# Opening loads issued step by step, ones multiplied on TensorE before the first features, and the last graph's softmax in thirds

## The chip, the cores and the metric

One core of one Trainium2 chip runs the whole program. The metric is the device time of one execution in microseconds (us). Engines are named as in the profile: PE (TensorE matmul) and PEld (its weight loads), DVE (VectorE), ACT (ScalarE), POOL (GpSimd), and SP (SyncE), which here issues every transfer.

## The reference

64 graphs of 128 nodes with 384 features go through four layers, each of the form x = x + layer(relu(layernorm(x))). Layers 0 and 2 are masked self-attention with 6 heads. Layers 1 and 3 are graph attention with 12 heads and a gate:

```python
h = einsum('bnd,ade->bane', feat, W); th = tanh(h)
attn = th @ w_src + swap(th @ w_dst)              # 12 heads, 128x128 each
attn = where(attn >= 0, attn, 0.2 * attn)
attn = softmax(where(adj, attn, -999.0))
out = elu(einsum('banm,bame->bane', attn, h) + b)
gate = sigmoid(feat @ H_w.T + H_b)
out = gate * out + (1 - gate) * feat
```

## The kernel before

A pair of layers (attention, then graph attention) is applied to one graph at a time. There are 2 pairs and 64 graphs, so 128 graph passes (`ALL = 128`), and they are software-pipelined: every engine's program is an unrolled loop over steps k from -7 to 132 (`run_steps`, L221), and in step k each engine does one stage each for graphs k+7 down to k-5. Every engine runs strictly in the order in which its program is written; between engines there are semaphores that count graphs. `r.has(g)` asks whether graph g exists, so the first steps and the last ones hold only some of the stages.

The stages that matter here, with the engine and the line:
- Statistics of the input of graph k+7 on DVE (L617 and L619); inverse deviation of graph k+5 on POOL (`layernorm`, L369); normalised features `hM` of graph k+4 on POOL (L411); their transpose on PE for graph k+5 of the step before (`features`, L721 to L724, called at L836); the high part `hT_hi` on ACT (L549) and the low part `hT_lo` on DVE (L655). DVE's order in step k puts the statistics of graph k+7 ahead of `hT_lo` of graph k+4.
- Queries and keys on PE for two graphs at once (`queries_keys`, L735, called at L771, L797 and L800; nine matmuls each). The first ones, in step -3, wait at L769 for `hT_lo` of graphs 0 and 1.
- Graph-attention scores of graph k-3: PE writes them into PSUM banks 5, 6 and 7, one bank for four heads (L812 to L815). ACT applies the leaky slope to all three banks in one instruction (L525), DVE writes the no-edge score (L636) and takes the maxima of the 12 heads (L640), ACT takes 12 exponentials, four per wait (`graph_exps`, L503, called at L555, L561 and L563), PE transposes them by fours (L787, L792, L805), ACT copies them (L520, L522, L534), and PE multiplies with the features (L862).
- The product goes through a 32x32 transpose on DVE (L652, `gcT`), four transfers to DRAM and one back (`context_back`, L269 to L279), and is then normalised on DVE (L625, two steps later than the scores' step). In step k DVE does: L625 for graph k-5, the reciprocal L632 for graph k-4, L636 and L640 for graph k-3, L652 for graph k-4. In step 130 that is: L625 of graph 125, L632 of 126, mask and maxima of 127, and L652 of 126. In step 131: L625 of 126, L632 of 127, L652 of 127.

Weights come as 14 pieces (`PIECES`, L145) of 192 or 288 KB through 8 staging slots. ACT rounds a piece to its high part (L584) and DVE subtracts to the low part (L692), in the steps of `SPLIT_STEPS` (L153). Pieces 8 to 13 reuse slots, so SP waits before each for the split of the piece eight before it (L250).

SP's opening order is written out at L281 to L302: features of graph 0, the identity, graph 1, pieces 0 to 5, bias columns, the first adjacency half, graph 2, pieces 6 and 7, graph 3, vectors of pair 0 (768 KB), head bias, one 576 KB matrix of pair 0 (`wf_stage[0]`), pieces 8 to 13, features of graphs 4 to 7, the second adjacency half, the matrix and the vectors of pair 1. Only then comes `straight(k)` for k from -2 on (L304, L352). `straight(-2)` waits for the copy of graph 0's features (`xb`, L343) and loads graph 8, `straight(-1)` the same for graphs 1 and 9; `straight(0)` and `straight(1)` send the head bias to DRAM and back. `xb` of graph 0 is POOL's (L406), in its step -1, behind the output bias of pair 0 (L481). PE reads the matrices of pair 0 and of pair 1 in its setup of step -2 and step 1 (L867 to L874).

PE's program starts with a wait for the identity (L710). The memsets of `ones` (a 128x128 tile, bf16) and others are POOL's first instructions (L360 to L367).

Of the kernel before, what the change touches and what calls it, by code (L numbers as in the profile page):

```python
# [32 lines left out]
NEG = -9000000000000000.0  # L33
NO_EDGE = -999.0
SLOPE = 0.2
# [6 lines left out]
HALF_SLOTS = SLOTS // 2  # L42
# [13 lines left out]
def graph_stack(nc, x, adj, w_qk, w_vf, w_hg, b_cols, vecs, h_b, ident, sel_src, sel_dst, out):  # L56
    B = x.shape[0]
    ALL = PAIRS * B

    with ExitStack() as ctx:  # L60
# [3 lines left out]
        def sem(name):  # L64
# [12 lines left out]
        vec = sb("vec", [128, PAIRS, 4, D])  # L77
# [72 lines left out]
                  ("gate", 2, D, COLS), ("gate", 2, D + COLS, COLS),  # L150
                  ("h", 2, 0, COLS), ("h", 2, COLS, COLS)]
        READY = {name: n + 1 for n, (name, _, _, _) in enumerate(PIECES)}
        SPLIT_STEPS = {-4: range(0, 3), -3: range(3, 6), -2: range(6, 8), -1: range(8, 11), 0: range(11, 14)}  # L153

        def whole(name):
# [9 lines left out]
        def bank(i):  # L165
            return psum[:, i, :]

        def banks(i, k):
            return psum[:, i:i + k, :]

        def chunks(ap):
# [9 lines left out]
            "cT_hi", "cT_lo", "o_ps", "x1",  # L181
            "g_stats", "g_mv", "g_var", "g_rstd", "g_shift", "g_h", "g_hT", "g_hi", "g_lo", "g_h_ps", "g_gate_ps",
            "g_th", "g_gate", "g_sigmoid", "g_haug", "g_prod", "g_sd", "g_sd_hi", "g_rest1", "g_sd_mid", "g_rest2", "g_sd3",
            "gc_out", "gc_back", "g_sdT_ps", "g_sdT", "g_sdR", "z_ps", "z_leaky", "z_masked", "z_max", "z_exp0", "z_exp1", "z_exp2",
            "gpt_ps0", "gpt_ps1", "gpt_ps2", "gpt0", "gpt1", "gpt2",
            "gc_ps", "gc", "pv_ps", "pv_rden", "pv_norm", "y_min", "y_exp", "ey_f", "xf", "elu_f", "mixed", "x2")}

# [44 lines left out]
        def _(sp):  # L232
# [3 lines left out]
            def load_x(src, g, slot):  # L236
                sp.dma_start(xin[:, slot:slot + 1, :], src[g:g + 1, :, :].rearrange("b p n -> p b n")).then_inc(x_in[slot], 16)

            def load_adj(g, half):
                sp.dma_start(adj8[:, half * HALF_SLOTS:(half + 1) * HALF_SLOTS, :],  # L240
                             adj[g:g + HALF_SLOTS, :, :].rearrange("b p n -> p b n")).then_inc(adj_in[half], 16)

            def load_piece(m):

                name, region, at, n = PIECES[m % len(PIECES)]
                if m >= len(PIECES) + 4:
                    j = m - len(PIECES) - 4
# [45 lines left out]
            sp.dma_start(vec[:, 0, :, :], vecs[0].partition_broadcast(128)).then_inc(s["vec_in0"], 16)  # L293
            sp.dma_start(hb_row[:], h_b.rearrange("k (a e) -> (k a) e", e=GD)).then_inc(s["hb_in"], 16)
            sp.dma_start(wf_stage[0], w_vf[0][:, D:2 * D].rearrange("(c p) n -> p c n", p=128)).then_inc(s["wf_in0"], 16)
            for m in range(8, len(PIECES)):
                load_piece(m)
            for i in range(4, SLOTS):
                load_x(x, i, i)
            load_adj(HALF_SLOTS, 1)  # L300
            sp.dma_start(wf_stage[1], w_vf[1][:, D:2 * D].rearrange("(c p) n -> p c n", p=128)).then_inc(s["wf_in1"], 16)
            sp.dma_start(vec[:, 1, :, :], vecs[1].partition_broadcast(128)).then_inc(s["vec_in1"], 16)  # L302

            def straight(k):  # L304

                if k == 0:
                    sp.wait_ge(s["hb_step"], 5)
                    sp.dma_start(hb_parts.rearrange("p (a e) -> a p e", e=GD), hb_part[:]).then_inc(s["hb_out"], 16)
                if k == 1:
                    sp.wait_ge(s["hb_out"], 16)  # L310
                    sp.dma_start(hb3[ROWS:ROWS + PARTS, :, :].rearrange("p k n -> p (k n)"), hb_parts).then_inc(s["hb_back"], 16)
                j, odd = divmod(k - AHEAD_STEP, SPREAD)
                if odd == 0 and 0 <= j < len(PIECES):
                    load_piece(len(PIECES) + j)
                if odd == 0 and 3 <= j < len(PIECES) + 3:
                    keep_piece(j - 3)
                for p in range(2):
                    if k == B - 3 + p + -1:
                        for i in [0, 2, 1]:
                            sp.wait_ge(s[f"qk_ps{i}"], B - 1 + p)  # L320
                            load_next(f"c{p}{i}")
                g = k - 4
                if 0 <= g < ALL:
                    context_back(g)
                if k == B - 2:
                    sp.wait_ge(s["m_v"], B)
                    load_next("V")
                g = k + 3
                if g % HALF_SLOTS == 0 and g >= SLOTS and g < ALL:
                    sp.wait_ge(s["masks"], g - HALF_SLOTS)  # L330
                    load_adj(g % B, g // HALF_SLOTS % 2)
                if k == B - 1:
                    sp.wait_ge(s["o_ps"], B)
                    load_next("O")
                g = k - 5
                if 0 <= g < ALL:
                    sp.wait_ge(s["x2"], g + 1)
                    slot = g % SLOTS
# [12 lines left out]

            for k in range(-2, ALL + 5):  # L352
                straight(k)
            for i in range(SLOTS):
                sp.wait_ge(stored[i], 16 * (ALL // SLOTS + 1))
# [137 lines left out]
        def _(act):  # L493
# [23 lines left out]
            def step(r, k):  # L517
# [4 lines left out]
                    act.activation(PTG[:, 1, :], bank(2), ACT.Copy).then_inc(s["gpt1"], 1)  # L522
                if r.has(k - 3):
                    act.wait_ge(s["z_ps"], r.done(k - 3))
                    act.activation(LG[:].rearrange("p (e n) -> p e n", e=3), banks(5, 3), ACT.Prelu, alpha=SLOPE).then_inc(s["z_leaky"], 1)  # L525
                if r.has(k + 2):
                    act.wait_ge(s["qk_ps1"], r.done(k + 2))
                    queries_keys(r, k, 1, bank(1)).then_inc(s["qk1"], 1)
# [22 lines left out]
                    act.wait_ge(s["g_hT"], r.done(k - 1))  # L551
                    act.activation(gT_hi[:], chunks(bank(0)), ACT.Copy).then_inc(s["g_hi"], 1)
                if r.has(k - 3):
                    act.wait_ge(s["z_max"], r.done(k - 3))
                    graph_exps(range(0, 4)).then_inc(s["z_exp0"], 1)  # L555
                if r.has(k):
                    act.wait_ge(s["c_ps"], r.done(k))
                    act.activation(cT_hi[:], chunks(bank(2)), ACT.Copy).then_inc(s["cT_hi"], 1)  # L558
                if r.has(k - 3):
                    act.wait_ge(s["z_max"], r.done(k - 3))  # L560
                    graph_exps(range(4, 8)).then_inc(s["z_exp1"], 1)  # L561
                    act.wait_ge(s["z_max"], r.done(k - 3))
                    graph_exps(range(8, 12)).then_inc(s["z_exp2"], 1)  # L563
                if r.has(k + 1):
                    act.wait_ge(s["m_v"], r.done(k + 1))
# [28 lines left out]
        def _(dve):  # L594
# [4 lines left out]
            def step(r, k):  # L599
# [31 lines left out]
                    wait_latest(dve, r, ("pv_norm", k - 6))  # L631
                    dve.reciprocal(rdenG[:, (k - 4) % 2, :], den[:]).then_inc(s["pv_rden"], 1)  # L632
                if r.has(k - 3):
                    dve.wait_ge(s["z_leaky"], r.done(k - 3))
                    dve.wait_ge(s["masks"], r.done(k - 3))
                    dve.copy_predicated(LG_heads, no_edge[:, (k - 3) % 2, :].unsqueeze(1).broadcast_to([128, GH, N]),  # L636
                                        no_edge_score[:].unsqueeze(2).broadcast_to([128, GH, N])).then_inc(s["z_masked"], 1)
                    dve.wait_ge(s["z_masked"], r.done(k - 3))
                    dve.wait_ge(s["z_masked"], r.done(k - 3))
                    dve.tensor_reduce(neg_max[:, 1, :], LG_heads, AX.X, ALU.max, negate=True).then_inc(s["z_max"], 1)  # L640
                if r.has(k + 1):
                    dve.wait_ge(s["s_ps"], r.done(k + 1))
                    dve.wait_ge(s["bias_mask"], r.done(k + 1))
# [65 lines left out]
        def _(pe):  # L709
# [154 lines left out]
                    last.then_inc(s["gc_ps"], 1)  # L864

            def setup(k):
                for pair, at in ((0, -2), (1, 0)):  # L867
                    if k == at:

                        pe.wait_ge(s[f"wf_in{pair}"], 16)  # L870
                        pe.wait_ge(s["bv_cols"], pair + 1)
                        for c in range(KC):
                            last = pe.matmul(bank(3)[:, 0:D], bv_cols[pair][:, c, :], wf_stage[pair][:, c, :], start=(c == 0), stop=(c == KC - 1))
                        last.then_inc(s["out_bias_ps"], 1)  # L874
                if k == 1:
                    pe.wait_ge(s["hb_back"], 16)
                    pe.nop(nofuse=True)
                if k == 2:
                    pe.wait_ge(s["setup_dve"], 2)
                    pe.nop(nofuse=True)  # L880

            run_steps(step, setup)


# [35 lines left out]
```

## Time and profile before

| what | value |
|---|---|
| median of 3 runs | 2048.41 us (2048.01 to 2048.42) |
| the profiled execution's own time | 2048.47 us |
| its span (first to last instruction of the trace) | 2046.4 us |
| busy share of the span | PE 97%, PEld 90%, DVE 89%, ACT 95%, POOL 80% |
| chain that ended last | ACT 49%, DVE 37%, PE 5% |

The span is shorter than the time by 2.07 us, which is what lies around the first and the last instruction. Times in views are microseconds from the span's start. In a timeline row the first number is the start, the second the duration, xN the number of instructions merged into the row, and the bracket says how long the engine had sat idle and what released it. In the chain of waits each row is a start, a duration, and whose instructions the time belongs to; DMA means that a transfer was being waited for.

### The profile page before, as it was taken

What the parts mean: (1) busy time and instruction counts of PE and PEld (TensorE: products, weight loads), DVE (VectorE), ACT (ScalarE), POOL (GpSimd) and SP (SyncE); (2) the same over time, 40 slices, a digit from 0 to 9 for tenths busy, and PEclk for the clock granted to TensorE, in tenths of its full rate; (3) what the DMA queues carried; (4) which work ended last, traced back from release to release, by engine and by line L of the source; (5) the groups of instructions that cost most, each with busy time, mean ns of one, the idle gap of its engine ahead of it and who ended that gap; (6) DMA issues with size and microseconds to landing.
All of it is one profiled execution on the core that took longest, in us unless ns stands there. A gap on an engine that the chain in (4) does not pass through costs nothing.

```text
span 2046.4 us, 58352 instructions
## 1 busy us (share of the span) xinstructions
PE 1979.5 (97%) x19596; PEld 1845.0 (90%) x19596; DVE 1813.4 (89%) x4117; ACT 1953.5 (95%) x6800; POOL 1629.2 (80%) x2859
## 2 busy tenths in 40 slices
PE   4999999999999999999999999999999999999983
PEld 4899999999999999999999999999999999999972
DVE  4689999999999999999999999999999999999884
ACT  3799999999999999999999999999999999999995
POOL 3478888888888888888888888878888878888864
PEclk9999999999999999999999999999999999999995
DMA  5012223323323222223432222222222222221122
GB/s 170 12 46 67 70 60 79 86 68 91 86 65 83 53 51 57 56 50 82 122 99 58 53 52 60 50 53 61 50 52 61 50 54 60 50 52 49 39 47 50
DMA packets 309330, 130.62 MB, mean 64 GB/s; under 512 B 229547, under 2 KB 308782, under 8 KB 309038
## 3 DMA queue, kind: packets, MB, share of 16 engines
q1 hardware_dynamic: 309038, 126.90, 24.8%
q8 instruction: 162, 2.65, 0.5%
q14 instruction: 130, 1.06, 0.2%
HBM read 69.42 MB, written 57.41 MB: 62 GB/s over the span
## 4 chain that ended last, share of the span: by engine, by line
ACT 49%; DVE 37%; PE 5%; issue 4%; POOL 2%; DMA 1%; DVEq 1%; SPq 1%; POOLq 0%
ACT LG L506 27%; ACT LA L500 14%; DVE LG L636 11%; DVE neg_max L640 10%; DVE LA L613 9%; DVE stats L617 3%; ACT cT_hi L558 2%; ACT QKT L514 2%; ACT v L566 2%; PE psum L731 2%; DVE rdenG L632 1%; DVE rden L611 1%; ACT sdT L572 1%; PE psum L741 1%; DMA xin<-x 1%
## 5 line engine op out<-in xcount | busy, mean ns | idle before, releaser
L506 ACT ACTIVATE LG<-LG,neg_max 128x128 f32<-128x128 f32 x1536 | 595.4, 392 | 15.9 <-DVE neg_max L640 8.8
L500 ACT ACTIVATE LA<-LA,neg_max 128x128 f32<-128x128 f32 x768 | 297.9, 400 | 0.0
L506 ACT ACTIVATION_READ_ACCUMULATOR LG<-LG,neg_max 128x1 f32 x1536 | 291.9, 190 | 0.0
L430 POOL TENSOR_TENSOR prod<-th,vec 128x384 f32<-128x384 f32 x256 | 254.3, 1017 | 6.9 <-ACT th L543 6.9
L636 DVE COPY_PREDICATED_SCALAR LG<-no_edge,no_edge_score 128x1536 f32 x128 | 245.5, 1918 | 7.4 <-ACT LG L525 7.3
L640 DVE TENSOR_REDUCE neg_max<-LG 128x12 f32<-128x1536 f32 x128 | 224.4, 1753 | 13.8
L741 PE MATMUL psum<-hT_hi,qk_hi 128*128 128x256 f32 x1152 | 212.4, 292 | 8.5 <-DVE hT_lo L655 8.5
L613 DVE TENSOR_TENSOR LA<-LA,rden 128x768 f32<-128x768 f32 x128 | 199.0, 1555 | 4.4
L741 PE MATMUL psum<-hT_hi,qk_lo 128*128 128x256 f32 x1152 | 200.8, 282 | 0.0
L741 PE MATMUL psum<-hT_lo,qk_hi 128*128 128x256 f32 x1152 | 200.6, 282 | 0.0
L525 ACT ACTIVATE LG<-psum 128x1536 f32<-128x1536 f32 x128 | 186.4, 1457 | 2.3 <-PE psum L814 2.3
L731 PE MATMUL psum<-hg_hi,gT_hi 128*128 128x384 f32 x768 | 188.4, 354 | 0.0
L375 POOL TENSOR_TENSOR rstd<-var_eps,minus_half 128x1 f32<-128x1 f32 x256 | 170.0, 664 | 21.3
L440 POOL TENSOR_TENSOR x<-y,x 128x384 f32<-128x384 f32 x128 | 128.9, 1007 | 69.9 <-DVE y L675 69.9
L645 DVE CUSTOM_DVE_ANT_0 LA<-psum,neg_bias 128x128 f32<-128x128 f32 x768 | 171.2, 285 | 12.9 <-PE psum L851 12.9
L741 PEld LDWEIGHTS psum<-hT_hi,qk_hi 128*128 128x128 f32 x1152 | 172.2, 190 | 9.3 <-DVE hT_lo L655 9.1
L731 PE MATMUL psum<-hg_lo,gT_hi 128*128 128x384 f32 x768 | 174.8, 336 | 0.0
L731 PE MATMUL psum<-hg_hi,gT_lo 128*128 128x384 f32 x768 | 174.6, 336 | 0.0
L411 POOL TENSOR_SCALAR hM<-xin,rstd,shift 128x384 f32<-128x384 f32 x128 | 168.7, 1318 | 4.6 <-PE psum L723 4.3
L741 PEld LDWEIGHTS psum<-hT_hi,qk_lo 128*128 128x128 f32 x1152 | 165.1, 189 | 0.0
L741 PEld LDWEIGHTS psum<-hT_lo,qk_hi 128*128 128x128 f32 x1152 | 164.7, 188 | 0.0
L678 DVE TENSOR_TENSOR sdR<-psum,sel 96x512 bf16<-96x512 bf16 x128 | 87.9, 687 | 77.0 <-ACT sdT L572 77.0
(121 smaller groups left out, 6201.5 us busy)
## 6 DMA issues: line engine op xcount, KB each, us to landing
context<-gcT SPq DMA_DIRECT2D x512, 48.0 KB, 2.1
back<-context SPq DMA_DIRECT2D x128, 192.0 KB, 2.5
xin<-x SPq DMA_DIRECT2D x64, 192.0 KB, 2.4
x_mid<-x SPq DMA_DIRECT2D x64, 192.0 KB, 2.4
xin<-x_mid SPq DMA_DIRECT2D x64, 192.0 KB, 2.4
out<-x SPq DMA_DIRECT2D x64, 192.0 KB, 2.3
ahead<-stage SPq DMA_DIRECT2D x16, 288.0 KB, 3.5
stage<-w_qk SPq DMA_DIRECT2D x12, 192.0 KB, 3.6
```

The lines of the kernel that those rows point to most:

```text
L375: pool.tensor_tensor(rstd[:, i, b:b + 1], var_eps[:, i, b:b + 1], minus_half[:], ALU.pow).then_inc(s[kind + "_rstd"], 1)
L411: pool.tensor_scalar(hM[:], xin[:, b, :], rstd[:, 0, b:b + 1], shift[:, 0, b:b + 1], ALU.mult, ALU.add).then_inc(s["m_h"], 1)
L430: last = pool.tensor_tensor(prod[:, i, :], th[:], vec[:, r.pair(k - 2), 2 + i, :], ALU.mult)
L500: last = act.activation(head, head, ACT.Exp, scale=-1.0, bias=neg_max[:, 0, h:h + 1], accum_out=rsum[:, h:h + 1])
L506: last = act.activation(head, head, ACT.Exp, bias=neg_max[:, 1, a:a + 1], accum_out=den[:, a:a + 1])
L525: act.activation(LG[:].rearrange("p (e n) -> p e n", e=3), banks(5, 3), ACT.Prelu, alpha=SLOPE).then_inc(s["z_leaky"], 1)
L613: dve.tensor_tensor(LA_heads, LA_heads, rden[:].unsqueeze(2).broadcast_to([128, MH, N]), ALU.mult).then_inc(s["p_norm"], 1)
L636: dve.copy_predicated(LG_heads, no_edge[:, (k - 3) % 2, :].unsqueeze(1).broadcast_to([128, GH, N]), no_edge_score[:].unsqueeze(2).broadcas ...
L640: dve.tensor_reduce(neg_max[:, 1, :], LG_heads, AX.X, ALU.max, negate=True).then_inc(s["z_max"], 1)
L645: last = dve.tensor_tensor_reduce(LA[:, i * N:(i + 1) * N], bank(4 + i // KC)[:, (i % KC) * N:(i % KC + 1) * N], neg_bias[:, (k + 1) % 2, ...
L731: last = pe.matmul(dst, a(c), w[:, c, at:at + D], start=(n == 0 and not begun), stop=(n == 3 * KC - 1))
L741: last = pe.matmul(dst[:, 0:2 * N], w[:, j, c * 128:(c + 1) * 128], a[:, j, g % 4:g % 4 + 2, :].rearrange("p b n -> p (b n)"), start=(m == ...
```

## The change

The loads behind `wf_stage[0]` are issued in `straight(k)`, which begins at k = -3: pieces 8, 9, 10 and the features of graphs 4 and 5 in step -3; pieces 11, 12, 13 and graph 6 in step -2, ahead of the wait for `xb` of graph 0; graph 7, the second adjacency half and the matrix and vectors of pair 1 in step -1, behind that wait. PE waits for the memsets, multiplies `ones` by `ones` 36 times before its first step, and 16 times in the setup of step -4, between the transposes of graphs 0 and 1. For the last graph pass (127) the leaky slope, the mask and the maxima are done for four heads at a time, and ACT's exponentials wait for their own third.

```diff
+        LOAD_STEP = [-3, -3, -3, -2, -2, -2]
...
-            for m in range(8, len(PIECES)):
-                load_piece(m)
-            for i in range(4, SLOTS):
-                load_x(x, i, i)
-            load_adj(HALF_SLOTS, 1)
-            sp.dma_start(wf_stage[1], ...).then_inc(s["wf_in1"], 16)
-            sp.dma_start(vec[:, 1, :, :], ...).then_inc(s["vec_in1"], 16)
             def straight(k):
+                for m in range(8, len(PIECES)):
+                    if k == LOAD_STEP[m - 8]:
+                        load_piece(m)
+                for i in range(4, SLOTS):
+                    if k == max(i + -8, -3):
+                        load_x(x, i, i)
+                if k == -1:
+                    load_adj(HALF_SLOTS, 1)
+                    sp.dma_start(wf_stage[1], ...).then_inc(s["wf_in1"], 16)
+                    sp.dma_start(vec[:, 1, :, :], ...).then_inc(s["vec_in1"], 16)
                 if k == 0:
...
-            for k in range(-2, ALL + 5):
+            for k in range(-3, ALL + 5):
                 straight(k)
...
 # ACT, graph k-3
-                    act.activation(LG[:]..., banks(5, 3), ACT.Prelu, alpha=SLOPE).then_inc(s["z_leaky"], 1)
+                    if k - 3 < ALL - 1:
+                        act.activation(LG[:]..., banks(5, 3), ACT.Prelu, alpha=SLOPE).then_inc(s["z_leaky"], 1)
+                    else:
+                        for q in range(QUADS):
+                            act.activation(LG[:, q * 4 * N:(q + 1) * 4 * N], bank(5 + q), ACT.Prelu, alpha=SLOPE).then_inc(s["z_leaky" if q == QUADS - 1 else f"last_leaky{q}"], 1)
...
-                    act.wait_ge(s["z_max"], r.done(k - 3))
+                    if k - 3 < ALL - 1:
+                        act.wait_ge(s["z_max"], r.done(k - 3))
+                    else:
+                        act.wait_ge(s["last_max0"], 1)
                     graph_exps(range(0, 4)).then_inc(s["z_exp0"], 1)
...
 # the same for heads 4 to 7 (last_max1) and 8 to 11 (last_max2); DVE, graph k-3
+                    else:
+                        dve.wait_ge(s["masks"], r.done(k - 3))
+                        for q in range(QUADS):
+                            heads = slice(4 * q, 4 * q + 4)
+                            if q == QUADS - 1:
+                                dve.wait_ge(s["z_leaky"], ALL)
+                            else:
+                                dve.wait_ge(s[f"last_leaky{q}"], 1)
+                            dve.copy_predicated(LG_heads[:, heads, :], ...).then_inc(s["last_masked"], 1)
+                            dve.wait_ge(s["last_masked"], q + 1)
+                            dve.tensor_reduce(neg_max[:, 1, heads], LG_heads[:, heads, :], AX.X, ALU.max, negate=True).then_inc(s[f"last_max{q}"], 1)
...
 # PE
             def setup(k):
+                if k == -4:
+                    warm_up(16)
...
+            def warm_up(n):
+
+                for _ in range(n):
+                    pe.matmul(bank(3)[:, 0:N], ones[:], ones[:], start=True, stop=True)
+
+            pe.wait_ge(s["ones"], 2)
+            warm_up(36)
             run_steps(step, setup)
```

## Rows read from the trace of the kernel before

**Rows 1.** The page: busy us, share of the span and instructions.

```profile
PE 1979.5 (97%) x19596; PEld 1845.0 (90%) x19596; DVE 1813.4 (89%) x4117; ACT 1953.5 (95%) x6800; POOL 1629.2 (80%) x2859
```

**Rows 2.** Timeline of the opening: POOL, PE, DVE, and PE again.

```profile
1.86 0.74 POOL L366 MEMSET hb<- 128x768 bf16 x1
...
6.87 0.87 PE L723 MATMUL psum<-idf,hM 128*128 128x128 f32 x3 [6.87 <-POOL hM L411]
...
16.27 0.87 PE L723 MATMUL psum<-idf,hM 128*128 128x128 f32 x3 [8.52 <-DVE hT_lo L655]
...
24.39 0.56 DVE L617 BATCH_NORM_STATS2 stats<-xin 128x6 f32<-128x384 f32 x1 [5.94 <-DMA xin<-x]
...
25.66 1.01 PE L741 MATMUL psum<-hT_hi,qk_hi 128*128 128x256 f32 x3 [8.52 <-DVE hT_lo L655]
...
30.43 0.49 PE L723 MATMUL psum<-idf,hM 128*128 128x128 f32 x3
...
37.79 0.55 PE L723 MATMUL psum<-idf,hM 128*128 128x128 f32 x3 [1.70 <-POOL hM L411]
...
49.69 2.20 PE L873 MATMUL psum<-PTG 128*128 128x384 f32 x6
```

**Rows 3.** Timeline of the opening: DMA issues of SP.

```profile
14.36 3.89 SPq L251 DMA_DIRECT2D stage<-w_hg  x4
18.29 2.23 SPq L237 DMA_DIRECT2D xin<-x  x4
...
37.11 3.78 SPq L237 DMA_DIRECT2D xin<-x  x2
```

**Rows 4.** Stretches: us, busy of each engine, PEclk, DMA share, GB/s.

```profile
15.00:24.00 9.00, 0.87 (x3) 0.50 (x3) 3.41 (x8) 0.49 (x1) 3.11 (x9) 1.00 1.08 348
...
40.00:41.00 1.00, 1.00 (x5) 1.00 (x4) 1.00 (x8) 0.00 (x0) 1.00 (x2) 0.50 0.00 0
```

**Rows 5.** The page: DMA issues, KB each, us to landing.

```profile
stage<-w_hg SPq DMA_DIRECT2D x8, 288.0 KB, 4.6
...
PTG<-w_vf SPq DMA_DIRECT2D x1, 576.0 KB, 6.9
```

**Rows 6.** The chain of waits in the opening.

```profile
39.20 3.17 PE psum L731 x9
...
52.68 1.76 PE psum L731 x9
...
67.84 2.15 PE psum L741 x18
```

**Rows 7.** Timeline near 70 us: the nearest bf16 weight load and matmul.

```profile
69.92 0.09 PEld L820 LDWEIGHTS psum<-hb,ones 32*128 32x128 bf16 x1
69.93 0.33 PE L820 MATMUL psum<-hb,ones 32*128 32x384 bf16 x1
```

**Rows 8.** Timeline of steps 130 and 131: ACT and DVE.

```profile
2018.06 1.45 ACT L525 ACTIVATE LG<-psum 128x1536 f32<-128x1536 f32 x1 [0.81 <-PE psum L814]
...
2019.55 1.96 DVE L636 COPY_PREDICATED_SCALAR LG<-no_edge,no_edge_score 128x1536 f32 x1 [0.94 <-ACT LG L525]
...
2019.89 0.53 ACT L540 ACTIVATE ey<-ey 128x384 f32<-128x384 f32 x1
...
2021.62 1.75 DVE L640 TENSOR_REDUCE neg_max<-LG 128x12 f32<-128x1536 f32 x1
2023.29 0.57 DVE L652 STREAM_TRANSPOSE gcT<-psum 128x384 f32<-128x384 f32 x1
2023.41 0.40 ACT L506 ACTIVATE LG<-LG,neg_max 128x128 f32<-128x128 f32 x1 [2.99 <-DVE neg_max L640]
...
2030.63 0.56 DVE L625 TENSOR_TENSOR y<-back,rdenG 128x384 f32<-128x384 f32 x1 [5.74 <-DMA back<-context]
2031.10 0.22 DVE L632 RECIPROCAL rdenG<-den 128x12 f32<-128x12 f32 x1
...
2031.78 0.58 DVE L652 STREAM_TRANSPOSE gcT<-psum 128x384 f32<-128x384 f32 x1 [0.45 <-PE psum L862]
```

More of the change, by code:

```diff
@@ L183, in graph_stack @@
             "g_th", "g_gate", "g_sigmoid", "g_haug", "g_prod", "g_sd", "g_sd_hi", "g_rest1", "g_sd_mid", "g_rest2", "g_sd3",
-            "gc_out", "gc_back", "g_sdT_ps", "g_sdT", "g_sdR", "z_ps", "z_leaky", "z_masked", "z_max", "z_exp0", "z_exp1", "z_exp2",
+            "gc_out", "gc_back", "g_sdT_ps", "g_sdT", "g_sdR", "z_ps", "z_leaky", "z_masked", "z_max", "last_leaky0", "last_leaky1", "last_masked", "last_max0", "last_max1", "last_max2", "z_exp0", "z_exp1", "z_exp2",
             "gpt_ps0", "gpt_ps1", "gpt_ps2", "gpt0", "gpt1", "gpt2",
@@ L295, in _ @@
             sp.dma_start(wf_stage[0], w_vf[0][:, D:2 * D].rearrange("(c p) n -> p c n", p=128)).then_inc(s["wf_in0"], 16)
-            for m in range(8, len(PIECES)):
-                load_piece(m)
-            for i in range(4, SLOTS):
-                load_x(x, i, i)
-            load_adj(HALF_SLOTS, 1)
-            sp.dma_start(wf_stage[1], w_vf[1][:, D:2 * D].rearrange("(c p) n -> p c n", p=128)).then_inc(s["wf_in1"], 16)
-            sp.dma_start(vec[:, 1, :, :], vecs[1].partition_broadcast(128)).then_inc(s["vec_in1"], 16)
-            def straight(k):
+            def straight(k):
+                for m in range(8, len(PIECES)):
[6 more added lines that the diff above has]
+                    load_adj(HALF_SLOTS, 1)
+                    sp.dma_start(wf_stage[1], w_vf[1][:, D:2 * D].rearrange("(c p) n -> p c n", p=128)).then_inc(s["wf_in1"], 16)
+                    sp.dma_start(vec[:, 1, :, :], vecs[1].partition_broadcast(128)).then_inc(s["vec_in1"], 16)
                 if k == 0:
@@ L524, in step @@
                     act.wait_ge(s["z_ps"], r.done(k - 3))
-                    act.activation(LG[:].rearrange("p (e n) -> p e n", e=3), banks(5, 3), ACT.Prelu, alpha=SLOPE).then_inc(s["z_leaky"], 1)
+                    if k - 3 < ALL - 1:
+                        act.activation(LG[:].rearrange("p (e n) -> p e n", e=3), banks(5, 3), ACT.Prelu, alpha=SLOPE).then_inc(s["z_leaky"], 1)
+                    else:
+                        for q in range(QUADS):
+                            act.activation(LG[:, q * 4 * N:(q + 1) * 4 * N], bank(5 + q), ACT.Prelu, alpha=SLOPE).then_inc(s["z_leaky" if q == QUADS - 1 else f"last_leaky{q}"], 1)
                 if r.has(k + 2):
@@ L559, in step @@
                 if r.has(k - 3):
-                    act.wait_ge(s["z_max"], r.done(k - 3))
+                    if k - 3 < ALL - 1:
+                        act.wait_ge(s["z_max"], r.done(k - 3))
+                    else:
+                        act.wait_ge(s["last_max1"], 1)
                     graph_exps(range(4, 8)).then_inc(s["z_exp1"], 1)
-                    act.wait_ge(s["z_max"], r.done(k - 3))
+                    if k - 3 < ALL - 1:
+                        act.wait_ge(s["z_max"], r.done(k - 3))
+                    else:
+                        act.wait_ge(s["last_max2"], 1)
                     graph_exps(range(8, 12)).then_inc(s["z_exp2"], 1)
@@ L633, in step @@
                 if r.has(k - 3):
[L634 to L640, printed above, removed]
+                    if k - 3 < ALL - 1:
+                        dve.wait_ge(s["z_leaky"], r.done(k - 3))
+                        dve.wait_ge(s["masks"], r.done(k - 3))
+                        dve.copy_predicated(LG_heads, no_edge[:, (k - 3) % 2, :].unsqueeze(1).broadcast_to([128, GH, N]),
+                                            no_edge_score[:].unsqueeze(2).broadcast_to([128, GH, N])).then_inc(s["z_masked"], 1)
+                        dve.wait_ge(s["z_masked"], r.done(k - 3))
+                        dve.wait_ge(s["z_masked"], r.done(k - 3))
+                        dve.tensor_reduce(neg_max[:, 1, :], LG_heads, AX.X, ALU.max, negate=True).then_inc(s["z_max"], 1)
+                    else:
+                        dve.wait_ge(s["masks"], r.done(k - 3))
+                        for q in range(QUADS):
+                            heads = slice(4 * q, 4 * q + 4)
+                            if q == QUADS - 1:
+                                dve.wait_ge(s["z_leaky"], ALL)
+                            else:
+                                dve.wait_ge(s[f"last_leaky{q}"], 1)
+                            dve.copy_predicated(LG_heads[:, heads, :], no_edge[:, (k - 3) % 2, :].unsqueeze(1).broadcast_to([128, 4, N]),
+                                                no_edge_score[:].unsqueeze(2).broadcast_to([128, 4, N])).then_inc(s["last_masked"], 1)
+                            dve.wait_ge(s["last_masked"], q + 1)
+                            dve.tensor_reduce(neg_max[:, 1, heads], LG_heads[:, heads, :], AX.X, ALU.max, negate=True).then_inc(s[f"last_max{q}"], 1)
                 if r.has(k + 1):
```

## The prediction

> **What bounds the kernel now.** The page comes first: PE is busy for 97% of the span and ACT for 95% [rows 1]. Between the opening and the last steps there is nothing to win here, because the change leaves those steps alone. Only two stretches can move, and they are read separately: the time until the first queries and keys, and the time after the last scores.
>
> For the opening I read the timeline and asked of each idle bracket what ended it. PE transposes the features of graphs 0 and 1 at 6.87 and 16.27, and begins real work at 25.66, after 8.52 us of idling for `hT_lo` [rows 2]. DVE is the engine that owes `hT_lo`, and it had itself sat 5.94 us in front of the statistics of graph 4, for a transfer that landed at 24.39 [rows 2]. The statistics are ahead of `hT_lo` in DVE's order, so a load that nobody needs for four steps holds the first matmuls. That load was issued at 18.29, behind all six pieces 8 to 13 [rows 3], and the 16 DMA engines were full for the whole of it: 348 GB/s at a share of 1.08 [rows 4]. The opening is bound by bytes ahead of graph 4, then by compute.
>
> For the end I read the timeline of the last scores. The slope, the mask and the maxima of graph 127 run one behind the other from 2018.06 to 2023.37; ACT idles 2.99 us and starts its exponentials at 2023.41 [rows 8]. That is the visible serial stretch. What decides the end, though, is the transpose `gcT` of graph 127 at 2031.78, since the transfers behind it have nothing beside them [rows 8]. Two things are due shortly before it: PE's product, which released it after 0.45 us of idling, and DVE's own earlier work, L625 of graph 126, which waited 5.74 us for a transfer and began at 2030.63 [rows 8]. So a second chain stands 1.15 us behind the first.
>
> **Part 1, the loads.** Pieces 8 to 10 stay ahead of graph 4; pieces 11, 12 and 13 go behind it. They are 288 KB each [rows 5], together 864 KB or 0.885 MB, and at 348 GB/s [rows 4] that is 2.54 us. Graph 4 should land at 24.39 - 2.54 = 21.85. SP can issue it early enough: the first of the four w_hg issues at 14.36 is piece 10, so graph 4 follows near 14.9, some 3.4 us before 18.29 [rows 3], and the backlog keeps the engines full until it lands. From there everything up to the first queries and keys is DVE work of fixed length (24.39 to 25.66), so PE starts at about 23.1. I take **-2.5 us**. The bounds: nothing, if landing does not follow the order of issue; -3.4 us, if it follows the issue time instead of the bytes.
>
> What is moved past what: pieces 11 to 13 are behind graphs 4 and 5, and are read by ACT only after the first queries and keys, ten microseconds later. Graph 6 has the same bytes ahead of it as before, and DVE takes it only in step -1. Graph 7, the second adjacency half, and the matrix and vectors of pair 1 are now behind SP's wait for `xb` of graph 0. That wait ended at 37.11 [rows 3], or 34.6 when all is 2.5 us earlier. With graph 8 ahead of it the matrix is issued about 2 us later, near 36.5, and a landing of 6.9 us [rows 5] gives 43.4. PE reads it at 49.69 [rows 2], so 47.2: cover 3.8 us. The small head-bias transfers queue behind the 1.3 MB of matrix and vectors, 1.34 MB / 348 GB/s = 3.9 us, so they land by about 43, also ahead of PE's setup of step 1. Cost 0.
>
> The Trainium skill ("DMA: Bandwidth & Descriptors", the section on queues, rings and completion order) says that completion is not first in, first out, because one transfer is split over up to 16 rings; by it part of the 864 KB may be replaced by later transfers and the gain shrinks. That is a rival below.
>
> **Part 2, the ones.** 52 matmuls of 128 columns with a weight load each. The nearest row is a bf16 matmul of 384 columns, 0.33 us, with a load of 0.09 [rows 7]. Bounds for one: 0.33 / 3 = 0.11 us at full clock, and 0.33 + 0.09 = 0.42 if load and matmul do not overlap. I take 0.11 at the high clock and twice that, 0.22, at the low one, since the weight loads overlap matmuls throughout this trace [rows 1]. 36 of them from 2.7 us, when the last memset has ended [rows 2], end between 6.7 and 10.6, where the transposes of graph 0 began at 6.87; 16 more add 1.8 to 3.5 us and end before 14.9. The transposes of graph 1 wait for `hT_lo` of graph 0 until 16.27 [rows 2]. So they are hidden: cost 0. Gain: I take 0 too. Between the last of the ones and 23.1 PE has almost nothing to do, as before.
>
> **The clock.** The first 27 matmuls of queries and keys take 4.77 us, from 25.66 to 30.43 [rows 2], where 18 later ones take 2.15 [rows 6] and 27 would take 3.2: part of them ran at the lower level, 1.2 GHz. Later PE idles for 1.70 us ahead of 37.79 [rows 2], and at 40 us the granted clock is 0.50 [rows 4]; nine matmuls take 3.17 us instead of 1.76 [rows 6]. Both stretches are on the chain. When the work moves by 2.5 us these low stretches may move relative to it. At the low pace all 27 first matmuls would take 27 x (2.15 / 18) x (3.17 / 1.76) = 5.8 us instead of 4.8: +1.0. If the second low stretch is missed: -1.4. I take 0 and keep both.
>
> **Part 3, thirds.** The slope in thirds frees the first third after about 0.5 us instead of 1.45, so DVE begins near 18.68 in place of 19.55 (2018.68 and 2019.55). Its work is now six instructions. Mask: 1.96 / 3 = 0.65 at the least, taken as 0.72; maxima: 1.75 / 3 = 0.58, taken as 0.62; and a wait of 0.1 us inside each third, as between 2021.51 and 2021.62 [rows 8]. Three thirds: 3 x 1.44 = 4.3, so DVE is through at 2023.0 instead of 2023.29, where it starts `gcT` of graph 126. ACT starts its exponentials near 2020.4, when L540 of graph 125 has ended [rows 8], instead of 2023.41, and since a third of exponentials takes longer than a third of DVE's work it runs through. PE's product of graph 127 comes 3.0 us sooner, near 2028.7. But `gcT` of graph 127 stands behind L625 of graph 126, and that one moves only with `gcT` of graph 126: 0.3 us. It starts at 2030.3, the reciprocal at 2030.8, `gcT` of 127 at 2031.0 instead of 2031.78. I take **-0.75 us**. The bounds: -0.45, if DVE's thirds cost as much as they bring; -1.1, if they cost nothing extra (0.87 us on an unchanged sum, less the wait); and -3.0 if I misread the second chain. What is late next is the transfer back of graph 126, the releaser of L625 at 2030.63 [rows 8].
>
> **Sum.** 2048.47 - 2.5 - 0.75 = 2045.2 in the profiled execution's own time, 0.06 above the median; from the median 2048.41 it is 2045.2 as well. A difference of 0.2%, or 4.1 us, is about what a measurement of this kernel can tell from none, so this forecast is a gain that counts as none.
>
> **The rivals.**
> - *Clock in its favour* (0.23). The second low stretch is missed, or the first matmuls run at the high clock. The missed stretch gives 1.4, 27 matmuls at 2.15 / 18 us would take 3.2 instead of 4.8 and give 1.6. One of them: 2043.7; both: 2042.2. For it: two low stretches are on the chain now. Against it: PE idled 8.5 us ahead of 25.66 and will idle as long behind the ones. By the Trainium skill ("TensorE: Matmul & The Clock Gate", on the HAM clock gate) low is the default and sustained activity lifts it, idling brings it back; by that the ones warm PE only for graph 0's transposes, and the sum stays.
> - *Clock against it* (0.16). All 27 first matmuls at the low level, the second stretch as before: +1.0, so 2046.2. For it: the first matmuls start earlier, and nothing says that the rise comes earlier too.
> - *Landing does not follow issue* (0.10). The pieces behind graph 4 share the rings with it as before; only the tail gains: 2047.7, at the least 2048.0.
> - *The tail gains its whole 3 us* (0.05): 2048.4 - 2.5 - 3.0 = 2042.9.
> - *Slower: the ones are in the way* (0.03). Graph 1's transposes must start by about 21.2 - so that ACT and DVE finish `hT_hi` and `hT_lo` by 23.1 - and 52 ones with graph 0's transposes (0.87) lie before them, from 2.7 on. They begin to decide when one costs (21.2 - 2.7 - 0.9) / 52 = 0.34 us, and the gain of part 1 is gone at 0.39. At the bound of 0.42 the first queries and keys start near 27.3, +1.7, and with the tail's -0.75 the time is 2049.4. Against it: weight loads lie beside matmuls in all rows of this trace.
> - The forecast itself has 0.43.
>
> **How the numbers follow.** The time is the likeliest case's, 2045.2. The range takes in the clock's favour with one stretch (2043.7) and, halfway, with both, so 2043.0; upward it takes the clock against it with a smaller gain of part 1, 2047.1. Left out: the landing rival (0.10), the slower one, half of the tail's. Faster by over 0.2% means below 2044.3: the favourable clock (0.23), the tail (0.05), and the upper end of part 1 and part 3 together (0.02) make 0.30. Slower by over 0.2% needs 2052.5, beyond the slower rival's own price, so it keeps 0.02. The rest, 0.68, is no difference.
>
> **What would show it.** In the changed trace: statistics of graph 4 at 21.5 to 22.2; first queries and keys at 23.1; the ones ended before 15 us and no idle bracket of PE that names them; `xb` of graph 0 and SP's next issue near 34.6; PE's setup of step 1 with no bracket for the matrix of pair 1. At the end: six DVE instructions in some 4.3 us, ACT's exponentials about 3 us nearer to the scores, and `gcT` of graph 127 with no idle bracket for PE, directly behind L632. The prediction is wrong if graph 4 lands after 23.5, if the second low stretch of the clock is gone or the first longer, or if `gcT` of graph 127 moves by over 1.2 us against the last scores.

## The result, and the profile after

| | median of 19 runs | lowest to highest |
|---|---|---|
| before | 2048.17 us | 2046.75 to 2049.08 |
| changed | 2044.87 us | 2043.48 to 2046.47 |

The ratio is 0.9984 with a 95% interval of 0.9978 to 0.9990: 3.3 us less (2.0 to 4.5), where 3.25 were forecast. The profiled execution of the changed kernel took 2046.47 us (span 2044.4), the slowest of the 19 and 1.6 us above their median; the marks below show where it spent its time. Line numbers of the changed kernel are higher: L617, L655, L741 and L723 of before are L634, L685, L771 and L753, L873 is L905, and L525, L636, L640, L652, L625, L632 are L533, L667, L670, L682, L642, L649.

The opening in the timeline of the changed kernel, the answer to [rows 2] and [rows 3] (the last row is from a narrower window, 34.4 to 35.5 us):

```profile
3.93 4.00 PE L917 MATMUL psum<-ones 128*128 128x128 bf16 x36 [3.93 <-DMA idf<-ident]
...
7.74 0.52 PE L753 MATMUL psum<-idf,hM 128*128 128x128 f32 x3
...
8.10 1.06 PE L917 MATMUL psum<-ones 128*128 128x128 bf16 x16
...
14.08 0.60 SPq L252 DMA_DIRECT2D stage<-w_hg  x1
...
14.73 1.02 SPq L238 DMA_DIRECT2D xin<-x  x2
...
16.23 0.87 PE L753 MATMUL psum<-idf,hM 128*128 128x128 f32 x3 [7.07 <-DVE hT_lo L685]
...
21.65 0.56 DVE L634 BATCH_NORM_STATS2 stats<-xin 128x6 f32<-128x384 f32 x1 [3.24 <-DMA xin<-x]
...
22.92 1.01 PE L771 MATMUL psum<-hT_hi,qk_hi 128*128 128x256 f32 x3 [5.82 <-DVE hT_lo L685]
...
28.60 0.49 PE L753 MATMUL psum<-idf,hM 128*128 128x128 f32 x3
...
34.74 0.82 SPq L238 DMA_DIRECT2D xin<-x  x2
```

Graph 4 is issued at 14.73 and lands 2.74 us sooner (21.65 against 24.39), and the first queries and keys start 2.74 us sooner. The ones are over at 9.16, and graph 1's transposes still wait for `hT_lo`. But the 27 first matmuls now take 5.68 us instead of 4.77. The stretches show the clock behind it (columns as in [rows 4]; the PEclk column is the one before the DMA share):

```profile
22.00:28.00 6.00, 5.08 (x24) 5.08 (x25) 2.82 (x7) 1.30 (x3) 0.00 (x0) 0.50 0.27 85
36.00:42.00 6.00, 5.83 (x48) 5.39 (x48) 3.88 (x16) 2.84 (x11) 5.31 (x10) 1.00 0.93 285
44.00:48.00 4.00, 3.81 (x23) 3.12 (x24) 1.76 (x12) 1.19 (x2) 0.66 (x1) 0.67 0.12 38
```

The first stretch is at 0.50, the 1.2 GHz level, for all of its six microseconds. The low stretch that before had near 40 us is gone (1.00), and another part of the opening, 44 to 48, has one instead.

One caution for the first microseconds of a trace: up to its first fall the PEclk column shows 1.00 whatever the pace. In the changed kernel it does so until about 11.2 us, although the first 36 ones start 0.106 us apart and the next 16 take 0.066 each. In the kernel before it shows 1.00 from 25 to 28 us, where groups of three matmuls start 0.64 us apart, just as they do at 0.50 here. So for the first matmuls the pace is compared, not the column.

```profile
25.00:28.00 3.00, 2.34 (x11) 2.34 (x12) 2.59 (x6) 0.01 (x1) 0.00 (x0) 1.00 1.00 362
```

The end, in the timeline of the changed kernel, answers to [rows 8]:

```profile
2016.80 1.57 ACT L533 ACTIVATE LG<-psum 128x512 f32<-128x512 f32 x3 [0.81 <-PE psum L844]
...
2017.51 0.79 DVE L667 COPY_PREDICATED_SCALAR LG<-no_edge,no_edge_score 128x512 f32 x1 [0.87 <-ACT LG L533]
...
2018.34 0.69 DVE L670 TENSOR_REDUCE neg_max<-LG 128x4 f32<-128x512 f32 x1
...
2018.94 0.79 DVE L667 COPY_PREDICATED_SCALAR LG<-no_edge,no_edge_score 128x512 f32 x1
...
2019.14 0.42 ACT L510 ACTIVATE LG<-LG,neg_max 128x128 f32<-128x128 f32 x1
...
2021.79 0.57 DVE L682 STREAM_TRANSPOSE gcT<-psum 128x384 f32<-128x384 f32 x1
...
2025.88 1.51 PE L892 MATMUL psum<-PTG,hv 128*32 128x128 f32 x24 [0.84 <-issue]
...
2029.15 0.56 DVE L642 TENSOR_TENSOR y<-back,rdenG 128x384 f32<-128x384 f32 x1 [5.76 <-DMA back<-context]
2029.62 0.22 DVE L649 RECIPROCAL rdenG<-den 128x12 f32<-128x12 f32 x1
2029.76 0.52 DVE L682 STREAM_TRANSPOSE gcT<-psum 128x384 f32<-128x384 f32 x1
```

Counted from the start of the last slope, the exponentials begin after 2.34 us instead of 5.35, and the last transpose `gcT` after 12.96 instead of 13.72. PE has ended its product at 2027.4; `gcT` has no bracket for PE any more. It stands directly behind the reciprocal (L649) and L642, and L642 had waited 5.76 us for graph 126's transfer. Three microseconds were won on ACT and PE, and 0.76 reached the end.

To see where the rest of the profiled execution went, the same instructions are marked in several traces (starts in us, from their timelines; the changed kernel is there twice, as it was profiled again as the last experiment):

| | before | changed | changed, again |
|---|---|---|---|
| first queries and keys | 25.66 | 22.92 | 22.07 |
| slope of graph 0 | 83.96 | 82.05 | 81.55 |
| slope of graph 124 | 1978.67 | 1976.63 | 1975.12 |
| slope of graph 127 | 2018.06 | 2016.80 | 2014.31 |
| normalisation of graph 127 | 2038.99 | 2036.97 | 2034.40 |

In the changed kernel's first profile the lead over before is 2.74 us at the first queries, 1.91 at graph 0's slope, 2.04 at graph 124's, 1.26 at graph 127's and 2.02 at the last normalisation. So 0.83 us of the new loads' gain is gone by graph 0's slope, where the first 27 matmuls had taken 0.91 longer; another 0.78 is lost in the last three steps (40.17 us where before needed 39.39); and the thirds bring 0.76.

The same kernel in its second profile is 2.6 us ahead of its first: 0.85 at the first queries (0.5 left at graph 0's slope), 1.0 in the long middle, and 1.0 in the last three steps (39.19 us). No row of the change is in the middle. So a single profile is good for the shape of an edit, and a time under 2 us is read from medians or from differences between two marks of one stretch.

### The profile page after: what moved, and what is told of

Read it like the earlier page. It is cut to its first block, busy times and chain, and to the rows that moved or that the text cites. A ratio compares the mean times of both kernels' runs of the same rounds, so it can differ in the third digit from the quotient of the medians.

```text
span 2044.4 us, 58461 instructions
## 1 busy us (share of the span) xinstructions
PE 1985.2 (97%) x19648; PEld 1850.5 (91%) x19648; DVE 1813.4 (89%) x4121; ACT 1953.4 (96%) x6802; POOL 1629.8 (80%) x2859
## 3 DMA queue, kind: packets, MB, share of 16 engines
q14 instruction: 130, 1.06, 0.2%
## 4 chain that ended last, share of the span: by engine, by line
ACT 50%; DVE 37%; PE 5%; issue 4%; POOL 2%; DMA 1%; DVEq 1%; SPq 0%; POOLq 0%
ACT LG L510 27%; ACT LA L504 14%; DVE LG L654 11%; DVE neg_max L658 10%; DVE LA L630 9%; DVE stats L634 3%; ACT cT_hi L569 2%; ACT v L583 2%; ACT QKT L518 2%; PE psum L761 2%; DVE rdenG L649 1%; DVE rden L628 1%; ACT sdT L589 1%; PE psum L771 1%; DVEq L215 1%
## 5 line engine op out<-in xcount | busy, mean ns | idle before, releaser
L771 PE MATMUL psum<-hT_hi,qk_hi 128*128 128x256 f32 x1152 | 212.6, 293 | 6.0 <-DVE hT_lo L685 6.0
L771 PE MATMUL psum<-hT_hi,qk_lo 128*128 128x256 f32 x1152 | 201.2, 283 | 0.0
L771 PE MATMUL psum<-hT_lo,qk_hi 128*128 128x256 f32 x1152 | 200.9, 282 | 0.0
L771 PEld LDWEIGHTS psum<-hT_hi,qk_hi 128*128 128x128 f32 x1152 | 172.1, 190 | 7.1 <-DVE hT_lo L685 6.9
L771 PEld LDWEIGHTS psum<-hT_hi,qk_lo 128*128 128x128 f32 x1152 | 165.5, 190 | 0.0
L771 PEld LDWEIGHTS psum<-hT_lo,qk_hi 128*128 128x128 f32 x1152 | 165.1, 189 | 0.0
```

Of the source, the lines that this page charges most:

```text
L771: last = pe.matmul(dst[:, 0:2 * N], w[:, j, c * 128:(c + 1) * 128], a[:, j, g % 4:g % 4 + 2, :].rearrange("p b n -> p (b n)"), start=(m == ...
```

## The experiments

Each kernel was timed beside the kernel before on the same chip, in 5 to 11 executions. The kernel before had medians of 2048.37 (first four), 2048.05 (next four) and 2048.46 us (last four).

**Without the ones.** The changed kernel less its ones:

```diff
-            pe.wait_ge(s["ones"], 2)
-            warm_up(36)
...
-                if k == -4:
-                    warm_up(16)
```

> The changed kernel without the 52 matmuls of ones. My theory: they are hidden and warm nothing that matters, so the first queries and keys still start at 22.9 us (changed kernel 22.92) and the time is that of the changed kernel within 0.5 us, about 3.3 us under the kernel before. Rival (the ones help): PE's first queries and keys, or the low stretch behind them, get longer without the ones, and the time is 1 to 1.6 us above the changed kernel's. Rival (the ones are in the way): it is faster than the changed kernel by over 0.5 us.

Measured: 2044.66 us, ratio 0.9983 (0.9974 to 0.9992). The same as the changed kernel. The first 27 matmuls took 4.95 us in its trace, and the start was at 21.98, because graph 4 had landed at 20.71 in that execution; the changed kernel with its ones had 20.80 in its second profile, so this is no effect of the ones.

**The new loads alone.** The thirds and the ones are left out of the changed kernel.

> The kernel before with the new order of loads alone. My theory: graph 4 lands at 21.6 to 21.9 instead of 24.39, the first queries and keys start near 23.0, the end is as in the kernel before (13.7 us from the last slope to the last 32x32 transpose, L652 of the kernel before), and the time is 2.5 us under the kernel before. Rival (the gain is lost in the steps between): the start moves by 2.7 us and the time by under 1 us.

Measured: 2046.63 us, ratio 0.9987 (0.9978 to 0.9996): 1.7 us less by the medians, 0.8 to 4.5 by the interval, which holds the 2.5. Its 11 executions fall into two groups, five at 2044.1 to 2044.9 and six at 2046.6 to 2047.4, so that the median lies in the upper one; by the means it is 2.7 us. Graph 4 landed at 21.86, the queries started at 23.14, and from the last slope to the last `gcT` it took 13.71 us, as before. The lead of 2.5 us at the queries was 1.7 at graph 0's slope (82.26), and this profile is one of the upper group.

**The thirds alone**, with the loads of before and no ones.

> The kernel before with the last graph's softmax in thirds alone. My theory: 13.0 us from the start of the last slope to the last 32x32 transpose instead of 13.7, so 0.7 to 0.8 us under the kernel before. Rival (the exponentials decide the end): 3 us under it.

Measured: 2047.51 us, ratio 0.9994 (0.9986 to 1.0003). The medians say 0.9 us less; the interval allows none. The trace is sharper: 12.90 us from the last slope to the last `gcT`, 0.8 less than before, and not 3.

**The ones alone**, with the loads and the softmax of before.

> The kernel before with the ones alone. My theory: first queries and keys at 25.7 us as before, at the lower clock level for the first of them (27 matmuls in 4.7 to 5.8 us), time within 0.5 us of the kernel before. Rival (the ones warm PE): the 27 take 3.2 us and the time is 1.5 us lower.

Measured: 2049.53 us, ratio 1.0003 (0.9994 to 1.0011). No gain. The median is 1.2 us up, outside the half microsecond expected, but its interval holds zero. The queries started at 24.92 and the 27 matmuls took 5.78 us.

The next four go beyond the change, to turn each reading into something that must show in the time.

**Graph 4 early.** Its load goes ahead of everything that the byte count says stands before it:

```diff
             load_x(x, 3, 3)
+            load_x(x, 4, 4)
...
-                for i in range(4, SLOTS):
+                for i in range(5, SLOTS):
```

> The changed kernel with the load of graph 4 issued right behind that of graph 3, ahead of the vectors, the matrix and pieces 8 to 10 as well. By the byte count (theory) it lands about 0.6 us behind graph 3, near 15.5 us; then DVE's own work up to 18.4 us is the limit, the first queries and keys start at 19.6 to 19.8 us instead of 22.9, and the time is 3.2 us under the changed kernel's. Rival (landing does not follow the order of issue): it lands after 18.5 us. Rival (the start is absorbed later, by the matrix or the pieces that now land later): the start is at 19.7, the time less than 1.5 us lower.

Measured: 2040.66 us, ratio 0.9965 (0.9952 to 0.9977), 4.2 us under the changed kernel. In the timeline DVE no longer waits for graph 4, and PE waits 2.48 us where it waited 5.82:

```profile
13.99 0.55 DVE L635 BATCH_NORM_STATS2 stats<-xin 128x6 f32<-128x384 f32 x1
17.44 0.55 DVE L635 BATCH_NORM_STATS2 stats<-xin 128x6 f32<-128x384 f32 x1
...
18.70 1.01 PE L772 MATMUL psum<-hT_hi,qk_hi 128*128 128x256 f32 x3 [2.48 <-DVE hT_lo L686]
```

The first row is graph 3, the second graph 4. The start is at 18.70, a microsecond better than expected, because graph 3 too was there before DVE asked for it (DVE began with it at 14.86 in the changed kernel's profile, after a wait). That is not the edit's doing: graph 3 was there in time in five of the nine traces that leave graph 4 in its later place, the changed kernel's second one among them. Against that one the start moves by 3.37 us, from 22.07 to 18.70, which is near the 3.2 expected. Issued early, graph 4 was there by 17.44, before DVE asked for it, and what is late next is DVE's own work.

**The last transposes swapped.** In step 131 DVE turns graph 127 before it normalises graph 126, and SP waits for that normalisation only ahead of the read back:

```diff
+                if k - 4 == ALL - 1:
+                    dve.wait_ge(s["gc_out"], 64 * r.done(k - 5))
+                    dve.wait_ge(s["gc_ps"], r.done(k - 4))
+                    dve.transpose(gcT[:], bank(7)[:, 0:D]).then_inc(s["gc"], 1)
                 if r.has(k - 5):
...
-                if g >= 1:
+                if 1 <= g < ALL - 1:
                     sp.wait_ge(s["pv_norm"], g)
...
                 sp.wait_ge(s["gc_out"], 64 * (g + 1))
+                if g == ALL - 1:
+                    sp.wait_ge(s["pv_norm"], g)
```

> The changed kernel with DVE's last 32x32 transpose (graph 127) put ahead of the normalisation of graph 126 in step 131, and SP's wait for that normalisation put behind the four transfers out instead of ahead of them. Theory (the end hangs on the transfers of graph 126): the transpose starts when PE's product is done, 10.6 to 10.8 us after the start of the last slope instead of 13.0, and the time is 2.2 us under the changed kernel's. Rival (SP or the transfers themselves are the limit): the transpose moves and the read back does not, and the time is the changed kernel's within 0.5 us.

Measured: 2042.00 us, ratio 0.9970 (0.9958 to 0.9982), 2.9 us under the changed kernel. Its timeline:

```profile
2025.43 1.51 PE L899 MATMUL psum<-PTG,hv 128*32 128x128 f32 x24 [0.84 <-issue]
...
2027.07 0.58 DVE L643 STREAM_TRANSPOSE gcT<-psum 128x384 f32<-128x384 f32 x1 [4.13 <-PE psum L899]
2027.68 2.56 SPq L278 DMA_DIRECT2D context<-gcT  x4
2028.61 0.56 DVE L649 TENSOR_TENSOR y<-back,rdenG 128x384 f32<-128x384 f32 x1 [0.96 <-DMA back<-context]
```

The last slope began at 2016.36, so `gcT` follows 10.71 us behind it, where it was 12.96. The bracket names PE again. Graph 127's normalisation comes 17.78 us after the slope instead of 20.17: 2.4 us, and the rest of the 2.9 is within the medians' own uncertainty. This shows that the second chain, graph 126's transfers, had kept back most of what the thirds gained.

**PE busy up to the first queries.** 64 more ones in the setup of step -3:

```diff
+                if k == -3:
+                    warm_up(64)
```

> The changed kernel with 64 more ones multiplied between the transposes of graph 1 and the first queries and keys, so that PE has no idle stretch there. Theory: the 27 first matmuls run at 2.4 GHz and take 3.2 us (5.7 in the changed kernel's trace), graph 2's transposes start at 26.2 instead of 28.6, and the time is 1.2 to 1.6 us lower. Rival (the chain goes through ACT and DVE behind the first of them, and PE's pace does not matter): the matmuls are shorter and the time is lower by under 0.5 us. Rival (the ones last too long at the low level and hold the queries back): these start after 23.5 us and nothing is gained.

Measured: 2043.59 us, ratio 0.9979 (0.9970 to 0.9988), 1.3 us under the changed kernel.

```profile
16.63 5.65 PE L919 MATMUL psum<-ones 128*128 128x128 bf16 x64
...
22.55 0.62 PE L771 MATMUL psum<-hT_hi,qk_hi 128*128 128x256 f32 x3 [0.26 <-DVE hT_lo L685]
...
25.88 0.49 PE L753 MATMUL psum<-idf,hM 128*128 128x128 f32 x3
```

The 27 matmuls take 3.33 us, 2.35 less than in the changed kernel's profile, and 1.3 reach the time. The stretch from 35 to 39 us is at a granted 0.66 here, so a low stretch behind the first one was not avoided.

**All three**, with 32 ones instead of 64, because the queries start earlier.

> The edits of the three kernels before it in one: graph 4 early, the last transposes swapped, and 32 ones ahead of the first queries and keys. If the three causes are separate the gains add: 3.2 + 2.2 + 1.4 = 6.8 us under the changed kernel's time, near 2038. If two of them share a limit, the sum is short by it.

Measured: 2037.47 us (2037.28 to 2038.20), ratio 0.9949 (0.9937 to 0.9962). It is the fastest kernel of this study, 10.6 us under the kernel before and 7.4 under the changed one. The single gains of 4.2, 2.9 and 1.3 would make 8.4. One shared limit is visible:

```profile
15.80 3.62 PE L927 MATMUL psum<-ones 128*128 128x128 bf16 x32
...
19.18 0.99 PE L779 MATMUL psum<-hT_hi,qk_hi 128*128 128x256 f32 x3
...
23.02 0.49 PE L761 MATMUL psum<-idf,hM 128*128 128x128 f32 x3
```

The queries have no bracket: PE was still at its ones when `hT_lo` was ready, and started half a microsecond later than with the early load alone (18.70). Yet 27 matmuls in 3.84 us, against 5.62 without those 32 (the kernel with the two edits, below), pay for it.

The last four runs separate these, and time the changed kernel again. **Early load and swap, without any ones:**

> The changed kernel with graph 4 early and the last transposes swapped, and without any ones. What is open: the kernels with the ones so far spend about 1 us more between the first queries and the last slope (1992.4 to 1994.2 us in their traces) than those without (1991.4 to 1992.9), while their medians do not agree on a sign. Theory (the ones cost nothing; that spread is from execution to execution): the median is within 0.5 us of the same kernel with the ones (next run). Rival (the ones cost 1 us): it is 1 us lower.

Measured: 2039.34 us, ratio 0.9955 (0.9943 to 0.9968). **The same with the change's own 52 ones:**

> The changed kernel, its 36 and 16 ones kept, with graph 4 early and the last transposes swapped. The two gains measured apart, 4.2 and 2.9 us, lie at opposite ends of the kernel and should add: 2044.9 - 7.1 = 2037.8 us. If they do not add, the two medians held luck of the clock.

Measured: 2039.68 us, ratio 0.9959 (0.9946 to 0.9971). The first 27 matmuls took 5.57 us without the ones and 5.62 with them. So the change's ones gain nothing. In all three comparisons of this study the kernel with them has the higher median, by 0.2, 0.3 and (the ones alone) 1.2 us, each within its noise, so that a cost of some tenths is not excluded. The two edits did not add up to 7.1 us but to 5.2 (5.4 against the changed kernel's second timing below). In the traces the swap is whole: 17.88 us from slope to normalisation, against 20.11 in the kernel with the early load alone. What differs is the first 27 matmuls, 5.62 against 5.04 us, and some tenths in the middle and in the last steps. So the medians of the early load alone and of the swap alone, from 5 and 6 runs, may have been about a microsecond lucky each; their intervals, 5 us wide, allow it, and the forecasts for the two, 3.2 and 2.2, add up to just 5.4. That is argued and not shown: no run separates it from a shared limit.

**The same with 18 more ones in step -3:**

> The run before with 18 more ones between graph 1's transposes and the first queries and keys. With 32 of them (3.62 us at the low level in the trace) PE was still at them when the queries could have started, 0.6 us late; 18 take 1.9 us at the low level and end before. Theory: the start is at 18.5 to 18.8, the clock rises sooner than without, and the median is 0.5 to 1 us under the run before. Rival (so short a stretch of ones in front does not bring the rise forward): the median is the same within 0.3 us.

Measured: 2039.82 us, ratio 0.9959 (0.9946 to 0.9973). No gain: the rival held. Whether 18 were too few or ended too early this run does not separate. They ended 0.57 us ahead of the queries, and these took 5.71 us:

```profile
16.06 2.12 PE L927 MATMUL psum<-ones 128*128 128x128 bf16 x18
...
18.75 1.01 PE L779 MATMUL psum<-hT_hi,qk_hi 128*128 128x256 f32 x3 [0.57 <-DVE hT_lo L693]
...
24.46 0.49 PE L761 MATMUL psum<-idf,hM 128*128 128x128 f32 x3
```

**The changed kernel again:**

> The changed kernel once more, as the yardstick of the three runs before it: 2044.9 us, within 0.5.

Measured: 2045.06 us, ratio 0.9983 (0.9974 to 0.9992).

## Why the prediction was right, point by point

- *Part 1, the loads: -2.5 us.* The byte count gave a landing at 21.85, and the changed kernel's profile has 21.65, the loads alone 21.86. The queries started at 22.92 against the forecast 23.1. The landing varies from execution to execution, and graph 3's with it. Where DVE had to wait for graph 3, graph 4 landed at 24.39 with the old order and at 21.65, 21.86 and 22.00 with the new one; where it had not, at 23.46 and 23.65 with the old and at 20.71, 20.80 and 21.27 with the new. That is 2.55 and 2.63 us between the means, where the bytes gave 2.54. The rival by which landing does not follow the order of issue is refuted for this load, most clearly by the early one. The Trainium skill ("DMA: Bandwidth & Descriptors", queues, rings and completion order) says that completion is not first in, first out. The traces show no case of it, but they show a landing only where an engine waits for it, and so can't rule it out.
- *How much of part 1 arrives.* The start moved by 2.74 us in the first profile, and 1.91 of it was left at graph 0's slope. The loads alone made 1.7 us by their medians and 2.7 by their means. So the 2.5 is shown for the start, and the time allows it, no more.
- *What was costed at nothing in part 1.* SP's next issue behind `xb` of graph 0, the load of graph 8, came at 34.74, where I had 34.6, and POOL's copy in that trace ended at 34.72 (33.71, 1.01 us). PE's setup of step 1 began at 46.91 against the forecast 47.2, with no idle bracket for the matrix of pair 1.
- *Part 2, the ones: 0.* Right in sum, and confirmed by taking them away twice. Two details were wrong. I let them start at 2.7 us, but PE's program waits for the identity first, and they started at 3.93. They pushed graph 0's transposes from 6.87 to 7.74, which ACT did not notice: it took their result at 10.77, before at 10.74. And both prices were too high: the first 36 took (7.74 - 3.93) / 36 = 0.106 us each, where the forecast had 0.22 for the low level, and the other 16 took 1.06 / 16 = 0.066, where it had 0.11 for the high one. Neither mattered, because the ones were hidden.
- *The clock: 0, with +1.0 and -1.4 as bounds.* This term did not come as forecast. The forecast named a longer first low stretch, or a second one that is gone, as signs that it is wrong, and the first profile shows both. The 27 matmuls took 5.68 us, where the rival had 5.8, and the low stretch at 40 us was missed. The miss gave nothing back, because the stretch at 44 to 48 us took its place, where PE's setup of step 1 took 3.10 us instead of 2.20; what the marks show is a loss of 0.83 us up to graph 0's slope. It is not tied to the change: the thirds alone, with the old loads and no ones, had 5.93 us for the same 27, and the changed kernel without its ones 4.95. What decides it from one execution to the next is open. The granted clock had fallen to 0.50 at about 11.2 us, 2 us after the last of the ones, and stayed there through the idling and graph 1's transposes until 28 us. By the Trainium skill ("TensorE: Matmul & The Clock Gate", the HAM clock gate) sustained activity lifts the clock and idling lowers it. The traces agree: under the 64 ones the granted clock rose from 0.50 to 1.00 between 20 and 22 us, and the 27 behind them took 3.33 us.
- *Part 3, the thirds: -0.75 us.* The trace has 13.72 - 12.96 = 0.76, the thirds alone 0.8. The first third of the mask began 0.71 us after the slope instead of 0.62, and DVE's six instructions took 4.28 us where 4.3 were worked out. The exponentials came 3.0 us sooner, as said, and were held by the second chain, as said. The swap proves the reading, since it frees 2.3 us more.
- *Sum.* 3.25 us forecast, 3.3 measured (2.0 to 4.5), and 3.4 in the repetition. The two mechanisms are shown, but that the sum fits this closely is luck: one execution differs from the next by up to 3 us, the clock moved by 0.8 where 0 was put down, and the single parts, each alone, add up by their medians (1.7, 0.9 and -1.2) to less than the whole, within intervals that are each about as wide as the gain.

## What to carry to other kernels

When an in-order engine owes a value and its idle bracket names a load that is needed only steps later, count the bytes issued ahead of that load and divide by the rate in the same stretch; that gives how much sooner it lands, here to 0.2 us. How much of this reaches the end is another question; here it was 1.9 of 2.74 us up to graph 0's slope. Before splitting a serial stretch for overlap, look for the second arrival at the point where the chains meet: the thirds won 3 us and kept 0.76, until the second chain was taken out of the way by an exchange of two instructions. Work that only keeps PE's clock up paid here where it lasted until the real matmuls began (64 and 32 ones); 52 that ended 13.8 us earlier and 18 that ended 0.57 us earlier gained nothing.

## What the runs showed that I had not expected

- 18 ones that end 0.57 us before the queries do not help at all, 64 that reach to within 0.26 us of them make 27 matmuls take 3.33 instead of 5.7 us, and 32 that overrun by half a microsecond still gain: 1.8 us against the kernel without them, each taken against the kernel before of its own chip (10.6 and 8.8 us). Number and gap changed together, so which of the two decides is open.
- The same load in the same program lands 0.85 us apart in two executions: graph 4 at 21.65 and 20.80 in the changed kernel. Over six traces with the same place for it the landing spans 20.71 to 22.00.
- Instructions on a third of the data cost more than a third: the mask 0.79 us for 512 columns against 1.96 for 1536, the maxima 0.69 against 1.75. Most of the excess overlaps with the next instruction, so that six of them took 4.28 us where two had taken 3.74.
